# Expert layer of a four-layer network: in each round of GpSimd's queue the scatter of an expert's outputs before the gather for the expert three ahead

## The reference, cut to what matters

```python
scores = softmax(flat_x @ gate_w.T).T            # T = 2048 tokens, E = 16 experts
topk_weight, topk_idx = top_k(scores, C)         # C = 2048 * 2 / 16 = 256 tokens for each expert
xg = flat_x[topk_idx]
h = gelu(xg @ Wg[e].T) * (xg @ Wu[e].T)          # hidden width 512
eo = (h @ Wd[e].T) * topk_weight[..., None]
out = zeros_like(flat_x).at[topk_idx].add(eo)
```

## Time and profile before

| | us |
|---|---|
| median of 3 runs | 1864.35 (1860.98 to 1866.83) |
| the profiled execution | 1873.98 |
| its span | 1872.2 |
| PE busy in the span | 1648.4 (88%) |
| DVE busy | 1313.8 (70%) |
| ACT busy | 1084.4 (58%) |
| POOL busy | 1081.7 (58%) |
| mean granted TensorE clock | 0.939 of full speed |

### The profile page before, as it was taken

The page is one execution under the profiler, slowest core; times in us unless marked ns, Lnnn a source line. Parts: engine busy times, 40 slices in busy tenths (PEclk is TensorE's granted clock), DMA queues, the critical chain, the costliest instruction groups (busy, mean ns, idle before and its releaser), DMA issues. The chain is left out here.

```text
span 1872.2 us, 32198 instructions
## 1 busy us (share of the span) xinstructions
PE 1648.4 (88%) x12270; PEld 1373.8 (73%) x12270; DVE 1313.8 (70%) x2730; ACT 1084.4 (58%) x2224; POOL 1081.7 (58%) x1022
## 2 busy tenths in 40 slices
PE   6999999999999999989976798965798468999897
PEld 4888888888888888878765677754577345666676
DVE  6888888888887888753454377758644588878882
ACT  3677767766666766645544455541433344666666
POOL 4888899999999999991045464633358610110111
PEclk9999999999999999999977999976799678999999
DMA  3000000000100000000013300030146300000000
GB/s 94 15 1 5 11 1 15 1 15 1 38 1 1 1 1 1 1 29 0 1 47 111 106 18 2 2 94 27 36 110 171 82 1 1 2 2 2 1 2 24
DMA packets 64089, 50.28 MB, mean 27 GB/s; under 512 B 10544, under 2 KB 55760, under 8 KB 63808
## 3 DMA queue, kind: packets, MB, share of 16 engines
q1 hardware_dynamic: 53328, 34.59, 6.3%
q0 software_dynamic: 8496, 12.59, 3.1%
q10 hardware_dynamic: 2112, 1.05, 0.2%
HBM read 37.72 MB, written 10.49 MB: 26 GB/s over the span
## 5 line engine op out<-in xcount | busy, mean ns | idle before, releaser
L756 POOL TENSOR_TENSOR dtl<-dts,dth 128x512 fp32r<-128x512 f32 x256 | 349.5, 1365 | 20.5
L686 DVE TENSOR_REDUCE nm<-PS 128x1 f32<-128x1024 f32 x256 | 311.2, 1216 | 23.4 <-PE PS L206 22.4
L2041 ACT ACTIVATE ET_a<-PS 128x256 f32<-128x256 f32 (+2 forms) x512 | 219.8, 498 | 123.4 <-PE PS L1954 78.2
L754 POOL CAST dth<-dts 128x512 fp32r<-128x512 f32 x256 | 237.5, 928 | 53.7 <-ACT dts L613 52.6
L204 PE MATMUL PS<-xh,yh 128*128 128x512 f32 x512 | 225.0, 440 | 10.7 <-ACT XNT L606 5.4
L147 PE MATMUL PS<-C,XN 128*128 128x128 f32 x1120 | 176.0, 283 | 40.6 <-DVE XN L199 37.8
L1853 POOL TENSOR_SCALAR_AFFINE_SELECT ET_a<-ET_a 128x1024 f32<-128x1024 f32 x32 | 34.9, 1092 | 302.8 <-ACT ET_a L2041 302.8
L206 PE MATMUL PS<-xh,yl 128*128 128x512 f32 x512 | 203.9, 398 | 0.0
L205 PE MATMUL PS<-xl,yh 128*128 128x512 f32 x512 | 203.7, 398 | 0.0
L606 ACT ACTIVATE XNT<-PS,nm 128x1024 f32<-128x1024 f32 x128 | 142.8, 1115 | 84.5 <-DVE nm L686 83.8
L613 ACT ACTIVATE dts<-PS 128x512 f32<-128x512 f32 x256 | 152.6, 598 | 49.2 <-POOL dtl L756 49.1
(11 more groups left out here) (419 smaller groups left out, 4265.1 us busy)
## 6 DMA issues: line engine op xcount, KB each, us to landing
e_wg<-in_WgT SPq DMA_DIRECT2D x16, 256.0 KB
e_wu<-in_WuT SPq DMA_DIRECT2D x16, 256.0 KB
e_wd<-in_WdT SPq DMA_DIRECT2D x16, 256.0 KB
m_x_rows<-m_xs SPq DMA_DIRECT2D x1, 1472.0 KB, 5.1
m_xs<-m_x_rows SPq DMA_DIRECT2D x5, 256.0 KB, 4.9
m_y_rows<-m_xs SPq DMA_DIRECT2D x5, 256.0 KB, 2.3
X<-in_L_attn_X SPq DMA_DIRECT2D x2, 512.0 KB, 4.7
wqn<-in_L_attn_Wq SPq DMA_DIRECT2D x8, 128.0 KB, 2.2
```

Of the source, the lines that this page charges most:

```text
L686: e.tensor_reduce(self.nm[:, half, i:i + 1], self.S[half], AX.X, MAX, negate=True).then_inc(*self.top.up((g, half)))
L754: e.tensor_copy(hi, src).then_inc(*ts.up((g, g4, "h")))
L756: e.tensor_tensor(lo, src, f(hi), SUB).then_inc(*ts.up((g, g4, "l")))
L2041: e.activation(dst, src, ACT.Exp, scale=self.SC, bias=0.0).then_inc(*self.ex.up(it))
```

## The change

Two lines move within the round. The loop issues s(x) first and g(x + 3) behind it; the root of round 7 stays ahead of s(7). Waits, buffers and all other engines' code are as before. The order on POOL becomes g0 g1 g2 s0 g3 s1 g4 s2 g5 and so on to s12 g15 s13 s14 s15.

```diff
         for x in range(3):
             gather(x)
         for x in range(self.E):
-            if x + 3 < self.E:
-                gather(x + 3)
             if x == 7:
                 k.rstd(e, q, self.ln2, self.ln2r, "x2")
             q.wait_ge(self.eo, (x, 1))
@@
             for h in range(2):
                 e.indirect_dma_start(self.yd[x % 2][:, :], bass.IndirectOffsetOnAxis(ap=self.IX[:, 2 * x + h:2 * x + h + 1], axis=0),
                                      self.EO[x % 2][:, h, :], None, compute_op=ADD).then_inc(*self.added[x % 2].up((x, h)))
+            if x + 3 < self.E:
+                gather(x + 3)
```

## The result

| | before | after |
|---|---|---|
| median of the runs | 1864.09 us (4 runs) | 1897.39 us (4 runs, 1892.91 to 1899.56) |
| profiled execution | 1873.98 | 1892.91 |
| its span | 1872.2 | 1891.1 |
| s0 to s15 | 95.22 | 124.21 |
| from s15 to the end of the span | 403.6 | 406.5 |

The ratio is 1.0176 with a 95% interval from 1.0158 to 1.0195: slower, by 33 us and not by the 15.2 that I had forecast, and outside the range. In the profiled executions the stretch from s0 to s15 grew by 29.0 us. The spans differ by 18.9 only, because s0 starts 13 us earlier in the one after (1360.3 against 1373.4), behind code that the change doesn't touch.

The account below looks back on a forecast made before the run. PE was busiest over the span, POOL's chain of scatters and gathers ruled the touched stretch, and PE set its end. Path +13.5 and clock +1.7 gave +15.2 on 1864.35: 1879.6 us, range 1869 to 1891.

Parts of the forecast that it names:

- the loop over two rounds: Scatter, gather, turn, down, scatter two rounds on: 13.83 us against POOL's own 12.80.
- s to second gather: On POOL, from the start of a scatter pair to the start of the gather's second transfer: 5.13 us.
- down to scatter: From PE's down of an expert to the start of its scatter on POOL: 2.89 us.
- L: Time from the start of a gather's second transfer until PE may turn: taken as 3.0 us, between 2.2 and 3.71.
- the path: Chain of steps from s0 to s15 in the new kernel: 108.75 us against 95.22 before, +13.5.
- a sign of being wrong: Listed contradictions in the changed profile: turns without waits, L outside 2.2 to 3.7, or POOL without pauses yet longer time.
- the pick: Extra work between turn and down: 5.07 us at turn(3), 5.46 at turn(7), instead of 2.81.
- The rival with the clock falling at every wait: Six experts of the path at half rate, 10.4 us: +23.9, 1888.3 us in total; chance 0.22.
- the clock term: PE's granted clock falls at one of the path's six waits, lengthening turn to down: +1.7 us.
- My own rival with both at their worst: Clock falling at every wait together with a gather landing of 3.71 us: 1892.6 us.
- the wait of `scale(x)` for a landing: Wait for s(x-2) to land, 6.4 us after it starts, while scale(x) comes 13 us after: costed at nothing.
- the weight loads' own lead: Weights asked for at each down and used three experts later, some 20 us: costed at nothing.

Follow-up runs that it names:

- Round 0 alone: Kernel before with only g3 put behind s0, then the order of before: 1875.84 us, ratio 1.0016, s0 to s15 98.8 us.
- the halves: Kernel before with the scatter first only in even rounds (1901.30 us, ratio 1.0138) or only in odd rounds (1888.73 us, ratio 1.0084).
- the two edits to the weights: Kernel after with weights asked for once the previous expert's gather landed (1893.47 us), or 1 in 32 weight columns loaded from expert 3 on (1891.21 us).
- Both edits together: Kernel after with weights asked for once the previous expert's gather landed, plus three extra matmuls before odd turns from 3: 1892.06 us, ratio 1.0087.
- eight buffers: Kernel before with eight gather buffers, g0 to g7 ahead of the loop, g(x+5) behind s(x) from x = 3: 1883.64 us, ratio 1.0036.
- the later weights: Kernel after, but weights of an expert asked for only once the previous expert's gather has landed: 1893.47 us, ratio 1.0094, s0 to s15 110.1 us.
- the filler: Kernel after with three extra 512-column matmuls on PE ahead of odd turns from 3: 1899.77 us, ratio 1.0120, s0 to s15 116.4 us.
- empty transfer engines: Kernel before with only 1 in 32 weight columns loaded from expert 3 on: s0 to s15 93.7 us, one run of 1876.6 us.
- the repeat of the kernel after: Kernel after, unchanged, run again beside the kernel before: 1900.31 us against 1872.87, ratio 1.0135, s0 to s15 125.1 us.

## Why the prediction was right or wrong

**Right**: the direction, the loop over two rounds through `eo`, gather, turn and down, and its order of events. s0 waits as before; s1 follows without a pause; s2 waits. s to second gather is 5.11 to 5.13 us in four of the steps where I had 5.13, and down to scatter 2.89 to 2.91 where I had 2.89. Round 0 alone, the halves and the two edits to the weights all came out within or at the edge of what this loop expects of the stretch. Both edits together (112.6 for 106 to 110) and eight buffers (92.7 for 88 to 91.5) did not.

**Wrong, first: the size of L.** I took 3.0, "nearest the middle row, since the gather will again follow a scatter and share with weight loads", and 3.71 as the upper bound. On the path it was 4.8, 4.2, 3.5, 4.5, 4.5, 4.0 and 2.7, five of seven outside the 2.2 to 3.7 that I had named as a sign of being wrong. My rows were not alike: the 2.2 was the end of the data in an idle stretch and not a start of PE, and no turn of any run here started less than 2.5 us after its transfer; g13's second transfer had started 2.2 us before the next load was asked for, g14's only 0.8. In the kernel before, that distance drifts from round to round. The loop fixes it: where PE doesn't wait it does down(x) and down(x+1) 5.46 us apart, the second asks for weights 4.5 us after s(x) started (four of six times; for g3 and g7 5.3 and 5.7, since there down(x+1) stopped for DVE), and the second gather transfer starts at 5.13. So six of the seven gathers of the loop meet a load, and the seventh, g15, for which there is no load, has 2.7. Against my 3.0 this makes 7.2 us over the seven waits (sum 28.2, less 21). The formula of the Trainium skill (page "DMA: Bandwidth & Descriptors", section "Anatomy of one DMA — SWDGE (gpsimd) path"), by which 2.2 us is an estimate for these bytes, stands near the 2.5 to 2.8 measured with the load out of the way; it has no term for the load.

**Wrong, second: the clock.** I spread the wait evenly, "1.5 us on average" for each expert, and counted one fall at 1.74. The loop makes PE do two experts without a pause and wait once for both, about 4 us. After five of the seven waits the half rate was there, and turn to down took 1.2 to 2.6 us longer. At turn(3), turn(5) and turn(9) the clock had dropped before PE resumed (for turn(5) 0.83 and 0.50 in the windows above, PE idle); at turn(11) and turn(13), behind waits just as long, it dropped only then, and cost 1.7 each. The length of the wait alone doesn't decide it: turn(15) waited 2.89 us without a fall, and with the later weights turn(10) waited 1.98 us with one. The five falls cost 9.7 us; at turn(7) the pick took 0.6 less than I had, which leaves 9.1 over the path instead of 1.7; the filler gave back up to 7.8. The rival with the clock falling at every wait was the nearest of my cases: it gave +23.9 and, with the long landing, +28.2. It had 0.22. The pattern behind it, which the Trainium skill describes (page "TensorE: Matmul & The Clock Gate", section "HAM oscillation — how this bites in real kernels"), is borne out by this trace for five of the seven turns, which started at half rate or fell to it soon after; the mean clock was 0.90.

**Small**: the path. With longer steps the even chain is also slower than POOL's pace and the root in the middle, so that seven waits lie on it and not six; 2.1 us of what I had counted as POOL's own pace there overlapped with it. s to second gather was 0.3 to 0.5 us longer in three steps, 1.2 us in all. Together 7.2 + 9.1 - 2.1 + 1.2 = 15.4, against the 15.5 by which the path (124.2) is longer than its working without the clock term (108.75).

**The range** ended at 1891, since it took 3.71 as the bound of L and gave the falling clock only in part. My own rival with both at their worst, 1892.6, lay outside it. The two terms came from the same waits and were both high together; I had treated them as independent. The loop explains the 29 us of the stretch; the 4 us between these and the 33 of the first whole runs stay open.

**Costed at nothing, rightly**: the wait of `scale(x)` for a landing and the weight loads' own lead. That lead was a resource: with the later weights seven of the twelve loads went out 1.6 to 3.7 us later, PE waited for none of them, and the stretch was 14 us shorter.

## What to carry to other kernels

When a request moves behind a wait, look for the loop that it closes and price it with the transfers that the loop itself sets off: the loop can lock them to one another, and a landing time from a trace without the loop is then too low (here 3.0 for 4.0 on average). A pause of TensorE can cost the pause and then the low clock behind it (here 1.2 to 2.6 us after five of seven), so ask whether the waits come as many short ones or as one long one. And a request that has lead to spare (here the weights) is better issued behind the one that has none, where something waits for that one; in the kernel before, where almost no gather is waited for, even empty transfer engines gained only 1.6 us.

## What the runs showed of the hardware

- A gather of 128 rows of 576 bytes took 2.5 to 3.0 us from the start of its issue to PE with the weight loads out of its way or cut to 1 in 32 columns, and 3.5 to 4.8 us beside 768 KB of loads (transfer engines busy to 0.87 to 1.05 in the three windows at g5).
- Matmuls whose result nobody reads, 2.6 us in a pause of 4, held the granted clock at 0.99 over 117 us (0.90 over 125 without them) and took 7.8 us off the stretch in one profile; beside the repeat of the kernel after, the gain of the whole program is not clear of the noise (1.0120 against 1.0135).
- With sixteen gather transfers instead of eight in a row in POOL's idle time, the stretch of the other engines beside them took 40.3 and 39.5 us instead of 32.2 (35 in three other kernels with six), with pauses whose releaser the profile doesn't know.
